# Query stage of a fused two-layer attention kernel: squares unsplit, low weight halves on GpSimd

## The reference, cut to what matters

```
def rms_norm(x, w, eps=EPS):
    xf = x.astype(jnp.float32)
    var = jnp.mean(xf * xf, axis=-1, keepdims=True)
    return w * (xf * jax.lax.rsqrt(var + eps)).astype(x.dtype)
...
q = (hidden_states @ Wq).reshape(B, S, N_HEADS, HEAD_DIM)   # 256 -> 16 heads of 128
...
q = rms_norm(q, q_norm_w)
```

## Time and profile before

| | us |
|---|---|
| median of 3 runs | 1384.92 |
| lowest and highest | 1380.15, 1387.37 |
| the profiled execution, its time | 1378.8 |
| the profiled execution, its span | 1376.4 |
| TensorE busy in the span | 1218.5 (89%) |
| VectorE | 917.0 (67%) |
| ScalarE | 738.8 (54%) |
| GpSimd | 530.6 (39%) |
| mean granted TensorE clock | 0.952 of full |

### The profile page before, as it was taken

One profiled execution on the slowest core, in us unless ns is written; L12 is line 12 of the kernel. 1 busy time (PEld: TensorE's weight loads), 2 busy tenths in 40 slices (PEclk: granted clock), 3 DMA queues, 4 the chain that ended last, 5 costly groups with the idle time before them and its releaser, 6 DMA issues. The chain is left out here.

```text
span 1376.4 us, 27058 instructions
## 1 busy us (share of the span) xinstructions
PE 1218.5 (89%) x9590; PEld 1046.8 (76%) x9590; DVE 917.0 (67%) x1895; ACT 738.8 (54%) x1256; POOL 530.6 (39%) x549
## 2 busy tenths in 40 slices
PE   4669999999999999999999569959999999957797
PEld 3438888888887888888888467848888888855686
DVE  5847888878778778888865854345665665543533
ACT  4636666576665766666564215434555555532542
POOL 2636353643636446354550425322212222200351
PEclk9869999999999999999999788979999999988799
DMA  4031111011110101110000600031111111005000
GB/s 149 1 90 46 45 46 46 6 40 45 45 45 23 65 2 45 45 40 5 0 1 1 219 0 1 0 97 47 31 45 45 32 42 45 1 10 201 1 1 14
DMA packets 34205, 57.13 MB, mean 42 GB/s; under 512 B 2802, under 2 KB 29794, under 8 KB 33634
## 3 DMA queue, kind: packets, MB, share of 16 engines
q1 hardware_dynamic: 34146, 56.35, 12.5%
HBM read 55.89 MB, written 0.46 MB: 41 GB/s over the span
## 5 line engine op out<-in xcount | busy, mean ns | idle before, releaser
L710 POOL TENSOR_TENSOR att_sq<-att_work,att_sq 128x500 fp32r<-128x500 f32 x96 | 127.2, 1325 | 177.0 <-DVE att_sq L608 177.0
L715 POOL TENSOR_TENSOR att_k<-att_work,att_k 128x500 fp32r<-128x500 f32 x96 | 129.8, 1352 | 159.1 <-DVE att_k L616 159.1
L97 PE MATMUL att_csum<-att_pT,att_cn 125*128 125x448 f32 x384 | 155.1, 404 | 1.3 <-DVE att_pT L654 0.4
L532 ACT ACTIVATE att_pr<-att_pr,att_nmx 112x1500 f32<-112x1500 f32 (+1 forms) x96 | 108.6, 1131 | 67.6 <-DVE att_nmx L645 67.6
L1466 POOL TENSOR_TENSOR kvs_ct<-kvs_raw,kvs_ct 128x1000 fp32r<-128x1000 f32 x24 | 56.4, 2352 | 224.1 <-ACT kvs_ct L1344 224.1
L99 PE MATMUL att_csum<-att_pT,att_cn 125*128 125x448 f32 x384 | 140.1, 365 | 0.0
L98 PE MATMUL att_csum<-att_pT,att_cn 125*128 125x448 f32 x384 | 139.5, 363 | 0.0
L654 DVE TENSOR_TENSOR att_pT<-att_ring,att_pT 125x448 fp32r<-125x448 f32 x192 | 118.4, 617 | 22.5 <-ACT att_pT L548 22.3
L642 DVE TENSOR_SCALAR_CACHE_REDUCE att_pr<-att_ring 112x500 f32<-112x500 f32 x192 | 120.7, 675 | 4.0 <-PE att_ring L99 2.3
L462 PEld LDWEIGHTS att_ring<-all_ident,att_pr 112*125 112x125 f32 x768 | 110.1, 189 | 14.3 <-ACT att_pr L532 2.2
L1285 PE MATMUL kvs_feat<-kvs_f,kvs_ks 128*125 128x256 f32 x768 | 112.1, 285 | 7.2 <-DVE kvs_kp L1434 5.6
(11 more groups left out here) (252 smaller groups left out, 3309.3 us busy)
## 6 DMA issues: line engine op xcount, KB each, us to landing
att_raw_n<-in_ctx SPq DMA_DIRECT2D x16, 750.0 KB
kvs_raw<-in_ctxT SPq DMA_DIRECT2D x24, 500.0 KB, 3.6
attention_raw_t<-in_ctxT SPq DMA_DIRECT2D x7, 1500.0 KB, 6.2
w_gate<-in_gate SPq DMA_DIRECT2D x1, 2112.0 KB, 8.6
w_up<-in_up SPq DMA_DIRECT2D x1, 2112.0 KB, 13.2
qry_raw<-in_wq SPq DMA_DIRECT2D x4, 512.0 KB, 5.7
wo_raw<-in_wo SPq DMA_DIRECT2D x4, 512.0 KB, 6.1
w_down<-in_down SPq DMA_DIRECT2D x1, 2048.0 KB, 18.3
```

The costliest lines, as they stand in the source:

```text
L97: nc.tensor.matmul(out, w_lo, x_hi, start=start, stop=False, skip_group_check=True)
L532: nc.scalar.activation(pr[:, j, keys], pr[:, j, keys], ACT.Exp, scale=-1.0, bias=nmx[:, j:j + 1], accum_out=z[:, 4 * u + j, c:c + 1]).then ...
L710: nc.gpsimd.tensor_tensor(sq[1][:, i % 2, :], work[:, i % 2, :], sq[0][:, i % 2, :].bitcast(F32), ALU.subtract).then_inc(sq_lo, 1)
L715: nc.gpsimd.tensor_tensor(k[1][x], work[:, i % 2, :], k[0][x].bitcast(F32), ALU.subtract).then_inc(k_lo, 1)
```

## The change

The squares are no longer split: ScalarE writes them in float32 into a tile of their own (`sq`, three buffers), and one plain float32 matmul a head takes their mean. With that VectorE's cast of the squares (L300) and GpSimd's subtraction (L311) go. The low halves of the query weights, so far the second instruction of VectorE's `split_w`, are made by GpSimd, in the place in its queue where the squares' low halves stood. Two waits change: the square waits for the mean of head h-3 (its buffer), and the logarithm, which now writes into `work` first, for the normalisation of head h-4.

```
--- before.py
+++ after.py
@@ -184,16 +184,16 @@
         wq = [p.sb(f"wq{i}", [128, DC, NH * HD], F32R) for i in range(2)]
         nw = p.sb("nw", [128, 4])
         eps = p.sb("eps", [128, 2])
-        mean_mat = p.sb("mean_mat", [128, 128], F32R)
+        mean_mat = p.sb("mean_mat", [128, 128])
         work = p.sb("work", [128, 4, NTOK])
-        sq = [p.sb(f"sq{i}", [128, 3, NTOK], F32R) for i in range(2)]
+        sq = p.sb("sq", [128, 3, NTOK])
         proj = p.ps("proj", [128, 4, 512])
         mean = p.ps("mean", [128, 2, 512])
         loaded = [p.sem(f"loaded{i}") for i in range(4)]
         next_loaded = [p.sem(f"next_loaded{i}") for i in range(len(splits))]
         w_hi, w_lo, next_hi, next_lo = (p.sem(s) for s in ("w_hi", "w_lo", "next_hi", "next_lo"))
-        nw_loaded, eps_set, nw_done, proj_done, sq_done, sq_hi, sq_lo, mean_done = (p.sem(s) for s in (
-            "nw_loaded", "eps_set", "nw_done", "proj_done", "sq_done", "sq_hi", "sq_lo", "mean_done"))
+        nw_loaded, eps_set, nw_done, proj_done, sq_done, mean_done = (p.sem(s) for s in (
+            "nw_loaded", "eps_set", "nw_done", "proj_done", "sq_done", "mean_done"))
         ln_done, rs_done, q_done = (p.sem(s) for s in ("ln_done", "rs_done", "q_done"))
         block = ctx.enter_context(nc.Block())
         QUARTER = NH // 4
@@ -219,12 +219,10 @@
             pe.wait_ge(eps_set, 3)
 
             def mean_square(h):
-                pe.wait_ge(sq_lo, h + 1)
+                pe.wait_ge(sq_done, h + 1)
                 wait(pe, ln_done, h - 1)
-                for half in (1, 0):
-                    last = nc.tensor.matmul(mean[:, h % 2, 0:NTOK], mean_mat[:], sq[half][:, h % 3, :],
-                                            start=(half == 1), stop=(half == 0))
-                last.then_inc(mean_done, 1)
+                nc.tensor.matmul(mean[:, h % 2, 0:NTOK], mean_mat[:], sq[:, h % 3, :],
+                                 start=True, stop=True).then_inc(mean_done, 1)
 
             for h in range(NH):
                 pe.wait_ge(w_lo, h + 1)
@@ -246,6 +244,7 @@
             def rstd(h):
 
                 act.wait_ge(mean_done, h + 1)
+                wait(act, q_done, h - 3)
                 nc.scalar.activation(work[:, h % 4, :], mean[:, h % 2, 0:NTOK], ACT.Ln,
                                      bias=eps[:, 0:1]).then_inc(ln_done, 1)
                 act.wait_ge(ln_done, h + 1)
@@ -254,8 +253,8 @@
 
             for h in range(NH):
                 act.wait_ge(proj_done, h + 1)
-                wait(act, q_done, h - 3)
-                nc.scalar.activation(work[:, h % 4, :], proj[:, h % 4, 0:NTOK], ACT.Square,
+                wait(act, mean_done, h - 2)
+                nc.scalar.activation(sq[:, h % 3, :], proj[:, h % 4, 0:NTOK], ACT.Square,
                                      bias=eps[:, 1:2]).then_inc(sq_done, 1)
                 if h >= 2:
                     rstd(h - 2)
@@ -270,16 +269,13 @@
         def _(dve):
             nc.vector.memset(eps[:, 0:1], RMS_EPS).then_inc(eps_set, 1)
             nc.vector.memset(eps[:, 1:2], 0.0).then_inc(eps_set, 1)
-            nc.vector.memset(mean_mat[:].bitcast(F32), 1.0 / HD).then_inc(eps_set, 1)
+            nc.vector.memset(mean_mat[:], 1.0 / HD).then_inc(eps_set, 1)
 
             def split_w(h):
 
                 if h % QUARTER == 0:
                     dve.wait_ge(loaded[h // QUARTER], 16)
                 nc.vector.tensor_copy(wq[0][:, :, head(h)], raw[:, :, head(h)]).then_inc(w_hi, 1)
-                dve.wait_ge(w_hi, h + 1)
-                nc.vector.tensor_tensor(wq[1][:, :, head(h)], raw[:, :, head(h)],
-                                        wq[0][:, :, head(h)].bitcast(F32), ALU.subtract).then_inc(w_lo, 1)
 
             def normalise(h):
                 dve.wait_ge(rs_done, h + 1)
@@ -295,9 +291,6 @@
             for h in range(NH):
                 if h + 2 < NH:
                     split_w(h + 2)
-                dve.wait_ge(sq_done, h + 1)
-                wait(dve, mean_done, h - 2)
-                nc.vector.tensor_copy(sq[0][:, h % 3, :], work[:, h % 4, :]).then_inc(sq_hi, 1)
                 if h >= 2:
                     normalise(h - 2)
             normalise(NH - 2)
@@ -307,9 +300,9 @@
         @block.gpsimd
         def _(pool):
             for h in range(NH):
-                pool.wait_ge(sq_hi, h + 1)
-                nc.gpsimd.tensor_tensor(sq[1][:, h % 3, :], work[:, h % 4, :], sq[0][:, h % 3, :].bitcast(F32),
-                                        ALU.subtract).then_inc(sq_lo, 1)
+                pool.wait_ge(w_hi, h + 1)
+                nc.gpsimd.tensor_tensor(wq[1][:, :, head(h)], raw[:, :, head(h)],
+                                        wq[0][:, :, head(h)].bitcast(F32), ALU.subtract).then_inc(w_lo, 1)
                 if h in NEXT_AT:
                     i = NEXT_AT[h]
                     pool.wait_ge(next_hi, i + 1)
```

## The result

The changed kernel takes 1411.56 us (median of 4 runs, 1404.96 to 1413.67), the kernel before 1384.14 us (4 runs too): a ratio of 1.0215, interval 1.0185 to 1.0245. The prediction was 1411, in a range of 1399 to 1423. The profiled execution has a span of 1411.2 us, 34.8 more than before.

A forecast was written before the change was run, and what follows sets the result against it. The query stage was taken as bound by TensorE's waits, to become a serial chain through GpSimd's queue: start to 29.7 us, four 12.2 us beats, 18.9 us tail, end 97.4 against 68.72, +28.7 us; 1411 us, range 1399 to 1423.

The forecast's parts named there:

- TensorE's head 4 waits for it: Query stage: head 4's low-half weights stand behind GpSimd's 2.4 us piece, so each copy starts a serial chain.
- The beat: Query stage, copy to copy over two heads: 12.2 us with half-clock restarts, against 6.32 us before.
- 4.7 us at half clock: TensorE's slow time after each of five restarts in the query stage, mean of 3.7 and 5.7 us.
- rival A: Query stage: clock stays full at the restarts, beat 9.9 us, stage end 85.8 us, +17.1 us; chance 0.19.
- Start and tail: Query stage's ends: first copy ends at 29.7 us instead of 29.13; tail 18.9 us against 14.9 before.
- VectorE's relief brings nothing here: Query stage: VectorE's removed casts and subtractions gain nothing, since VectorE is no longer what is late.
- Rival C: Query stage: piece not on the chain, ScalarE sets a 5.1 us beat, -4 us, 1381 us; chance 0.06.
- 2.02 a round: ScalarE's round in the query stage; two rounds and a 1.04 us copy make Rival C's 5.1 us beat.
- four beats save 4.9 us: Rival C's gain in the query stage's middle; start and tail give some 1 us back.
- The ports: VectorE's casts meeting GpSimd's weight subtractions at their shared ports in the query stage: 0, at most 1.5 us.
- Later stages unchanged: Sign that the forecast is right: stages after the query stage stay as before.

The follow-up runs named there:

- e1: Changed kernel with only GpSimd's queue reordered: low halves of the query weights made two heads ahead of the pieces; 1373.41 us, ratio 0.9956 to the kernel before.
- e2: Changed kernel with GpSimd's queue reordered so that the weights' low halves are made only one head ahead; 1397.14 us, ratio 1.0119 to the kernel before.
- e3: Changed kernel with the weights' low halves back on VectorE, keeping unsplit squares and the plain float32 mean; 1369.89 us, ratio 0.9926 to the kernel before.
- e4: Changed kernel plus 26 useless matmuls behind the mean in each of rounds 3, 5, 7, 9 and 11; 1399.14 us, ratio 1.0132 to the kernel before.
- e7: The changed kernel run once more, unaltered, on the chip of the later runs; 1412.22 us, ratio 1.0226 to the kernel before.
- e5: Kernel before with only the weights' low halves moved to GpSimd's serial queue place, squares still split; 1432.27 us, ratio 1.0387 to the kernel before.
- e8: e5 plus one tiny unused memset behind each of VectorE's 16 weight casts in the query stage; 1404.13 us, ratio 1.0184 to the kernel before.
- e9: e3 with the copies for the next stage's five pieces moved from ScalarE to VectorE; 1377.88 us, ratio 0.9974 to the kernel before.

## Why the prediction was right

**The wait.** "TensorE's head 4 waits for it" was the step that decided, and it was right: 27.1 us of waiting for L304 in the five restarts, a releaser that the kernel before did not have. e1 and e2 show that the order in the queue is the cause, and hardly the engine that does the work: two heads of slack remove all but 3.5 us of what separates the changed kernel from e3, one removes about half of the stage's loss.

**The beat.** Forecast 12.2 us, measured 11.59, 12.52, 11.45 and 12.46 from the end of one copy to that of the next. The waits in it are 5.4 to 5.5 us where 5.9 were forecast. The prediction took 4.7 us at half clock after each restart. The rows of the five restarts give 4.1 and 6.1 us in turn (33.47 to 37.6, 45.06 to 51.2, and so on), a mean of 4.9. The short ones are the first, third and fifth, and the beats alternate with them.

**The clock.** Full clock would have been rival A, with a beat of 9.9 us. e4 is that rival made real: 9.7 us, and a stage that ends at 85.87 us (85.8 in the rival).

**Start and tail.** First copy at 30.32 us (29.7 forecast), fifth at 78.34 (78.5), tail 18.1 us (18.9), end of the stage 96.45 (97.4). Start and the other two parts missed in opposite directions: 0.6 us too short, 0.8 (the beats) and 0.8 (the tail) too long. Of the tail's 0.8 us, 0.6 had been gained by the square of head 13 (86.80 us, 8.46 after the copy, 9.05 forecast), since this restart was one of the short ones; the rest is ScalarE's pitch, below.

**Luck in the number.** The stage was forecast at +28.7 us and came at +27.7. That the median came within 0.6 us of 1411 is luck: the forecast is a value chosen between 1407.5 and 1413.6, and the four runs themselves lie between 1404.96 and 1413.67.

**Where it was too confident or missed something.** "VectorE's relief brings nothing here" holds for the changed kernel only: e3 shows that it is worth 11 us once the weights are not behind the pieces. The change is thus a gain of 11 us and a loss of 38, and of these the order in the queue is some 35: e1, with the weights still on GpSimd, is 3.5 us above e3. Rival C priced the good case at 5.1 us a beat and -4 us in all; e1, which is C made real, has 4.9 us in the mean and -7.4, e3 has 4.55 us and -10.9. Two steps are at fault. ScalarE's "2.02 a round" adds record lengths, and its records overlap when nothing is waited for (1.75 a round in e3). And start and tail were to give 1 us back, where e3's tail is 11.3 us against 14.9, a gain of 3.6. C's "four beats save 4.9 us" is also 0.6 too much by the prediction's own numbers: four of 5.1 are 20.4, against 24.7. The ports were put at nothing, and were nothing here: GpSimd's pieces even fell from 2.43 to 2.34 us. "Later stages unchanged" did not hold in the profile: 7.1 us lie outside the stage, and why the readout lost its clock stays open. The cast of round h stands ahead of the normalisation of head h-2 in VectorE's queue and not behind it, which changes nothing in the sum. The medians differ by 27.4 us here and by 31.0 in e7, so 7 us more or less would not have changed the way the result went.

## What to carry to other kernels

When work moves to another engine, place it in that engine's queue before asking how long it takes: here 0.73 us of work behind one wait cost 7 us a beat, and the same work two rounds earlier cost 3.5 us in the whole stage. TensorE may also come back from such a wait at half clock (all five waits of 5.4 us here, one of five waits of 2.5 to 3.5 us in e2), so a serial wait should be priced with its restart at both levels. And a change of two halves should be run as halves: one of these was worth keeping.

## What the runs showed of the hardware

- Sixteen VectorE instructions more or less ahead of a loop changed its time by 28 us (e5 1432.27, e8 1404.13): in e5 each turn from the third on had VectorE idle for 3.5 us and the instruction queue q14 moved 48 packets in all instead of 23. That the loop's instructions are loaded anew at each turn fits this but was not shown; where the boundary lies was not tried.
- 130 matmuls of no use made the kernel 12 us faster (e4); the bursts behind them began at 2.4 GHz (first matmul 0.47 us) and not at 1.2 (0.74).
- ScalarE's instructions of 128x448 have records of 0.62 to 0.67 us and start 0.52 to 0.65 us apart when nothing holds them up (e3), so their lengths can't be added.
- VectorE's subtraction of two float32 operands lasted 2.44 us instead of 0.42 whenever GpSimd had begun a long one shortly before (e9). The Trainium skill ("SBUF — State Buffer", Who interferes with whom) describes this as an exclusive lock; the rows agree, also in that VectorE's normalisation, which has one operand in SBUF and the other in PSUM, is not held up (0.68 us beside a piece in e3).
